# Moving the remainders of the context rows from GpSimd to VectorE in the keys-and-values stage of a two-layer attention kernel

## The reference

```python
# feed-forward of layer 0: weights rounded to -1, 0, 1
gamma_w = jnp.clip(jnp.mean(jnp.abs(w)), 1e-05, None)
w_dq = jnp.clip(jnp.round(w / gamma_w), -1.0, 1.0) * gamma_w
...
# attention of layer 1
k = (encoder_hidden_states @ Wk + bk).reshape(b, se, NKV, HD).transpose(0, 2, 1, 3)
v = (encoder_hidden_states @ Wv + bv).reshape(b, se, NKV, HD).transpose(0, 2, 1, 3)
k = _rmsnorm(k, kn_w)      # x * rsqrt(mean(x * x) + 1e-6) * w over the 128 numbers of a head
```

## Time and profile before

| what | value |
|---|---|
| median of 3 runs | 1779.12 us |
| the profiled execution, its own time | 1780.04 us |
| its span (first to last instruction) | 1778.1 us |
| mean granted TensorE clock | 0.991 |
| TensorE busy over the span | 1707.0 us (96%) |
| VectorE busy | 1242.4 us (70%) |
| ScalarE busy | 924.0 us (52%) |
| GpSimd busy | 594.6 us (33%) |
| L785, lo on GpSimd | 14 instructions, first start 315.1 us, last start 397.3 us |
| between 342 and 396 us, each 6 us | TensorE busy 5.71 to 5.72, VectorE 5.34 to 5.38, ScalarE 3.71 to 4.18 us |

### The profile page before, as it was taken

The page is one execution under the profiler, slowest core; times in us unless marked ns, Lnnn a source line. Parts: engine busy times, 40 slices in busy tenths (PEclk is TensorE's granted clock), DMA queues, the critical chain, the costliest instruction groups (busy, mean ns, idle before and its releaser), DMA issues. The chain is left out here.

```text
span 1778.1 us, 26445 instructions
## 1 busy us (share of the span) xinstructions
PE 1707.0 (96%) x9562; PEld 1392.2 (78%) x9582; DVE 1242.4 (70%) x2313; ACT 924.0 (52%) x1774; POOL 594.6 (33%) x469
## 2 busy tenths in 40 slices
PE   7999998997999979999999999999899999999998
PEld 6998997774444458888788788878777799999876
DVE  5444443786888768888788788888768567767555
ACT  4443342564566466666666666666331365656411
POOL 3111143233677632221222212121210255555342
PEclk9999999998999999999999999999999999999999
DMA  9323210854143572121232222110161579797573
GB/s 319 93 86 103 76 49 4 305 207 136 36 95 75 149 234 92 61 84 60 89 104 88 87 63 84 60 60 1 49 252 59 190 247 306 256 305 251 191 245 108
DMA packets 175564, 238.25 MB, mean 134 GB/s; under 512 B 51270, under 2 KB 112454, under 8 KB 173254
## 3 DMA queue, kind: packets, MB, share of 16 engines
q1 hardware_dynamic: 156620, 203.14, 35.0%
q0 software_dynamic: 9600, 33.30, 6.0%
q10 hardware_dynamic: 9216, 0.14, 0.3%
HBM read 184.24 MB, written 43.78 MB: 128 GB/s over the span
## 5 line engine op out<-in xcount | busy, mean ns | idle before, releaser
L1233 POOL TENSOR_TENSOR a_rq<-a_ssq,a_qhalf 128x4 f32<-128x4 f32 x64 | 66.1, 1033 | 358.9 <-DMA a_ssq<-a_sum_row 358.9
L78 PE MATMUL bank<-a_xT_hi,a_wq_lo 128*128 128x512 f32 (+1 forms) x384 | 144.5, 376 | 1.4 <-DVE a_xT_lo L503 1.4
L80 PE MATMUL bank<-a_xT_hi,a_wq_hi 128*128 128x512 f32 (+1 forms) x384 | 139.0, 362 | 0.0
L79 PE MATMUL bank<-a_xT_lo,a_wq_hi 128*128 128x512 f32 (+1 forms) x384 | 138.4, 361 | 0.0
L78 PE MATMUL bank<-a_wo_hi,a_oT_lo 128*128 128x512 f32 x320 | 127.4, 398 | 5.9 <-POOL a_wo_lo L1246 4.1
L1396 ACT ACTIVATE a_scores<-a_scores,a_nmax 128x256 f32<-128x256 f32 x256 | 126.9, 512 | 0.8 <-DVE a_nmax L1573 0.8
L80 PE MATMUL bank<-a_wo_hi,a_oT_hi 128*128 128x512 f32 x320 | 125.7, 393 | 0.0
L79 PE MATMUL bank<-a_wo_lo,a_oT_hi 128*128 128x512 f32 x320 | 125.7, 393 | 0.0
L2123 POOL TENSOR_TENSOR e_wg_lo<-raw_g,e_wg_hi 128x1408 fp32r<-128x1408 f32 x25 | 87.9, 3516 | 112.3 <-ACT e_wg_hi L2195 112.3
L1385 ACT ACTIVATE a_sum_row<-bank,a_sum_eps 1x512 f32<-1x512 f32 x64 | 43.3, 677 | 142.3 <-PE bank L1765 142.3
L1273 POOL TENSOR_TENSOR f_h<-f_vv,f_gs 128x512 f32<-128x512 f32 x64 | 92.7, 1452 | 60.4 <-DVE f_vv L1503 59.7
(11 more groups left out here) (423 smaller groups left out, 5403.1 us busy)
## 6 DMA issues: line engine op xcount, KB each, us to landing
raw_g<-in_egw SPq DMA_DIRECT2D x26, 704.0 KB, 4.8
raw_u<-in_euw SPq DMA_DIRECT2D x26, 704.0 KB, 6.2
a_xT_hi<-x1T_hi SPq DMA_DIRECT2D x16, 1024.0 KB, 6.1
a_xT_lo<-x1T_lo SPq DMA_DIRECT2D x16, 1024.0 KB, 8.2
raw_d<-in_edw SPq DMA_DIRECT2D x26, 512.0 KB, 5.8
y_routed<-m_y SPq DMA_DIRECT2D x39, 256.0 KB, 6.7
raw_d<-in_edw SPq DMA_DIRECT2D x26, 192.0 KB, 6.7
a_cTraw<-in_ctxT SPq DMA_DIRECT2D x8, 512.0 KB, 5.8
```

The lines of the kernel that those rows point to most:

```text
L78: pe.matmul(out, w[1], x[0], start=first, stop=False)
L79: pe.matmul(out, w[0], x[1], start=False, stop=False)
L80: return pe.matmul(out, w[0], x[0], start=False, stop=last)
L1233: pool.tensor_tensor(rq[:, h % HG, :], ssq[u % 2][:], qhalf[:], ALU.pow).then_inc(s_rq, 1)
```

## The change

GpSimd no longer makes lo. VectorE makes it in its turn, two tiles ahead: in turn t, after `values_out` of tile t-1 and before `summed` of tile t, it makes lo of tile t+2, for t up to 13. The instruction, its operands, its wait for hi and the semaphore that it raises are the same. GpSimd keeps the stores.

```diff
         @block.gpsimd
         def _(pool):
-            def context_lo(t):
-                pool.wait_ge(s_chi, t + 1 - READY)
-                src = cTraw[t // QT % 2][:, :, t % QT * P:(t % QT + 1) * P]
-                pool.tensor_tensor(cT[t % 3].lo[:], src, f32(cT[t % 3].hi[:]), ALU.subtract).then_inc(s_clo, 1)
-
...
             pool.memset(eps_rms[:], RMS_EPS).then_inc(s_const, 1)
-            context_lo(READY)
             for t in range(T):
-                if t + 3 < T:
-                    context_lo(t + 3)
                 if t >= 3 and t % 2:
                     store((t - 3) // 2)
...
         @block.vector
         def _(dve):
+            def context_lo(t):
+                dve.wait_ge(s_chi, t + 1 - READY)
+                src = cTraw[t // QT % 2][:, :, t % QT * P:(t % QT + 1) * P]
+                dve.tensor_tensor(cT[t % 3].lo[:], src, f32(cT[t % 3].hi[:]), ALU.subtract).then_inc(s_clo, 1)
+
...
                 biased(t)
                 if t >= 1:
                     values_out(t - 1)
+                if t + READY < T:
+                    context_lo(t + READY)
                 summed(t)
```

## The result

The changed kernel takes 1770.75 us (median of 5 runs, 1770.09 to 1773.89) against 1779.84 us for the kernel before beside it (5 runs). The ratio is 0.9949, 95% interval 0.9938 to 0.9961: 9.1 us less, where 9.6 less were forecast from 1779.12. It was launched in two more groups of runs, where it gained 7.3 us (ratio 0.9958, 0.9945 to 0.9971) and 9.7 us (0.9952, 0.9939 to 0.9966).

A forecast was written before the change was run, and what follows sets the result against it. VectorE's queue was taken to set the pace, 6.47 us a turn, with steps held up by GpSimd. Terms -0.98, -8.3, -0.97, +0.43 and +0.2 gave -9.6 us: 1769.5 us, range 1767.3 to 1775.5.

The forecast's parts named there:

- The reason of the long step: VectorE's second `ternary` step, 1.41 us for 0.43, is shut out until GpSimd's remainder ends: 0.98 us lost, 11 times.
- The price of lo: Lo on VectorE mostly fills idle gaps: +0.15 us in each of turns 2 to 11, +0.43 in turn 13.
- the rival: Lo lies fully on VectorE's path, 0.61 us in 13 turns: only -3.6 us, 1775.5; chance 12%.
- The margin is at least 2.1 us: Stores: needed 8.5 us after issue, landing in 4.4 us, 6.4 at most, so VectorE's values would not wait.
- the delay of SyncE's wait: SyncE's context load waits for lo, ready 2 us later; ScalarE needs it two turns on, so costed at nothing.
- TensorE next: TensorE, 5.93 us a tile, binds next after VectorE's 5.64 us turn, limiting any gain beyond the sum to about 1 us.
- Stores too late: Rival: GpSimd's store issues are starved and values wait at the staging buffer, at worst +5.4 us, 1774.9; chance 4%.
- The start of the stage: Stretch from the stage's first VectorE instruction to turn 1, forecast to change by 0 us.
- no more than about 1 us beyond: Gain possible beyond the stage's -9.6 us, since VectorE runs only 4 to 1 us later than TensorE.
- Its barrier passes the gain on: Nothing after the stage is tied to an absolute time, so the full 9.6 us reaches the kernel's end.
- The whole: Whole kernel's time: 1780.04 - 9.6 = 1770.4, or 1769.5 from the median; own range 1767.5 to 1772.5 at 70%.

The follow-up runs named there:

- e3: Changed kernel, with GpSimd also making the remainder where it did before and VectorE writing lo again: 1785.98 us, ratio 1.0037 to the kernel before.
- e4: Changed kernel, with GpSimd only filling lo's tile with zeros at the remainder's old place, VectorE overwriting it: 1781.79 us, ratio 1.0010.
- e5: Kernel before, lo still on GpSimd but held until VectorE's second ternary step is done, stores issued ahead of it: 1768.94 us, ratio 0.9941.
- e1: Changed kernel, with VectorE's lo cut to 4 of 512 columns from tile 3 on: 1768.96 us, ratio 0.9937.
- e2: Changed kernel, with VectorE making each lo twice in a row: 1780.53 us, ratio 1.0006.
- e8: Changed kernel, with only an eighth of each weight piece loaded from the ninth on: 1770.50 us, ratio 0.9948.
- e6: Changed kernel, with SyncE issuing each context block's load one weight piece later: 1771.07 us, ratio 0.9949.
- e7: Kernel before, with lo on GpSimd held behind the second ternary step, stores ahead of it, and context loads one piece later: 1769.81 us, ratio 0.9948.
- e9: Kernel before, with GpSimd's lo held behind the second ternary step and stores ahead of it, launched again in another group: 1769.35 us, ratio 0.9947.

## Why the prediction was right, step by step

- **The reason of the long step** was right, and is shown by e3 (put back, it returns), e4 (a shorter GpSimd instruction makes a shorter loss, and the step ends 0.28 us after it, 0.29 in the earlier trace rows) and e5 (timed apart, it is gone). Its size, 0.98 in eleven turns and 0.97 in turn 12, was measured to 0.01.
- **The price of lo,** 0.15 a turn and 0.43 in turn 13: measured 0.14 (e1) and 0.41. The count of which part of it fills idle time held. e2 shows the bound that I used for the rival: once the idle places are filled, lo costs its full step and more.
- **"The margin is at least 2.1 us"** for the stores failed. I took the landing time from the trace of before as if it were a property of the store. It is one of the moment: the change put the issue of the store among the weight loads, and these now go out closer together, and one landing took 9.5 us for 6.4. That the loads are the cause is shown by e8; whether the new moment of the store or the denser loads weigh more is not shown (in e3 the store kept its place and landed after 10.9 us; in e6 and e7 the loads were spread out again and landings still took 8.8 and 9.6). The trace before had a sign of it: context load and four pieces, 2.5 MB, from 335.19 on, and the key store behind them. I had costed the delay of SyncE's wait at nothing since ScalarE needs that block late; what else it meets on the DMA engines I didn't ask. Turns 2 to 11 are longer by it by 2.4, 1.9 and 1.3 us in the three profiles; in the length of the stage it is at most the 1.2 to 1.8 us by which it stands above e1 and e5 to e9 (see "TensorE next").
- **"Stores too late"** as a rival thus holds in part, by another mechanism than the one I gave it. The rule on descriptor writing in the Trainium skill, page "SBUF — State Buffer", section "SBUF: two separate sides", played no part that the runs show: with the same fast steps of VectorE beside them, e8's issues took 0.55 to 0.78 us and every key store landed within 5.5. The 620 and 3100 ns that the Trainium skill gives there are, besides, said of a DMA from GpSimd's queue, not of its issue alone. And I misread the row that I set against it. The 0.77 us of the issue at 341.50 are no effect of the long second step: the issues at 354.43 and 367.35 also start beside one and take 0.57, and the first issue in the changed kernel (327.28) takes 0.77 beside none.
- **The start of the stage** I took as unchanged, but L944 collided too and lost 0.84 us. What the whole stretch gained is not to be told from its scatter (13.57 us before; 12.99, 13.31 and 13.72 after).
- **TensorE next,** "no more than about 1 us beyond": right, and closer than the text says. By its own numbers the keys of tile 15 start at 398.5 and end 2.73 later, at 401.3 (the text has 398.5 as their end), 0.3 us ahead of VectorE's 401.6, so that a stage of 107.06 - 9.6 = 97.5 us could shrink by a few tenths only. In the six profiles of e1 and e5 to e9 the stage takes 97.1 to 97.3 us, at different lengths of VectorE's turns, and TensorE no longer waits for the last scaled keys: one floor, 1.2 to 1.8 us below the three profiles of the changed kernel, where it waits 0.95 to 1.18.
- **"Its barrier passes the gain on"** is right to about 1 us: the next stage lost 0.8 to 1.1 us at the lower clock. In e1, e2 and e5 to e9 the low stretch around the barrier was only 6.8 us long; what decides between 6.8 and 10.2 was not tried.
- **The whole.** The stage gives 8.2 to 8.5 us, the next takes 0.8 to 1.1 back: 7.0 to 7.7. The medians say 7.3, 9.1 and 9.7. The stages ahead, with the same instructions, ended anywhere between 306.2 and 310.0 us in the profiles, so the rest is within what one profile cannot tell; the forecast's closeness in the whole is in part luck.

## What to carry to other kernels

When an instruction of one form shows two durations in a trace, look at what the other engines started just ahead of its long cases, and where those ended: the loss may be removed by timing the two apart as well as by moving the work. Work moved to the engine that sets the pace is cheap only where that engine has idle time of its size, so write its turn out start by start. And when the change moves an issue of a DMA or a wait in the load queue, look up what is on the DMA engines at its new moment, before a landing time is carried over.

## What the runs showed of the hardware

- VectorE's bf16 step of 128x1024, started behind a GpSimd instruction, was held until that had ended: 0.43 us became 1.41 beside a read-and-write of 1.29, and 0.71 beside a fill that only writes (0.62). The step ended 0.27 to 0.29 us after GpSimd. The other way round, GpSimd's remainder took 1.85 us for 1.29 where the first step of `ternary` started with it (326.79, before), and the fill 1.03 for 0.53 (323.92, e4).
- Additions that read a bank did not collide with the same GpSimd instruction (e5), nor did a reduction in the 0.14 us that it lay beside it.
- A VectorE product of one column with both inputs in SBUF took 1.00 us for 0.16 beside GpSimd's remainder (before), and 0.16 beside a fill (e4).
- A store of 512 KB took 3.3 us from issue to landing where no other transfer ran (issue at 403.94, before), and 9.5 us among 2.5 MB of loads (after).
- The stretch of low TensorE clock around one and the same barrier was 6.8 us long in the seven profiles of e1, e2 and e5 to e9 and 10.2 in the six others.
